# Register loads of one table entry per item, and TensorE's expert load between its two products, in a mixture-of-experts and attention kernel

## The reference

```python
x = x + 0.5 * ffn(layernorm(x))
x = x + attention(layernorm(x))          # 16 heads of 8, causal, rotary positions
x = x + 0.5 * ffn(layernorm(x))
```

```python
probs = softmax(xt @ Wr + br); gates = max(probs); idx = argmax(probs)      # per token
xn = layernorm(xt) * ln_g + ln_b
h = relu(xn @ W1[idx] + b1[idx])          # W1: 8 x 128 x 512
y = (h @ W2[idx] + b2[idx]) * gates       # W2: 8 x 512 x 128
```

## Time and profile before

| | us |
|---|---|
| runs of the kernel | 908.14, 914.18, 915.40 |
| median | 914.18 |
| span of the profiled execution | 855.6 |
| first item loop, in the profiled execution | about 44 to 132 |
| second item loop | about 759 to 846 |

### The profile page before, as it was taken

The page is one execution under the profiler, slowest core; times in us unless marked ns, Lnnn a source line. Parts: engine busy times, 40 slices in busy tenths (PEclk is TensorE's granted clock), DMA queues, the critical chain, the costliest instruction groups (busy, mean ns, idle before and its releaser), DMA issues. The chain is left out here.

```text
span 855.6 us, 17846 instructions
## 1 busy us (share of the span) xinstructions
PE 779.7 (91%) x5570; PEld 427.9 (50%) x5570; DVE 610.9 (71%) x1919; ACT 507.4 (59%) x1229; POOL 315.4 (37%) x603
## 2 busy tenths in 40 slices
PE   9889999887899999999999999999999997689995
PEld 8888896543233333333333333333333335579884
DVE  4657774698668777788878878788787722856663
ACT  2166651673247767667667766766777684146662
POOL 6177742475104223223322422331242231056753
PEclk8699999998569999999999999999999998789998
DMA  8721113065332033033113303312320001122110
GB/s 271 270 57 50 54 33 117 23 169 159 57 57 45 14 57 57 10 49 58 34 26 57 53 6 57 58 22 36 57 41 18 3 1 34 73 70 50 52 42 26
DMA packets 27989, 51.84 MB, mean 61 GB/s; under 512 B 7552, under 2 KB 19200, under 8 KB 26496
## 3 DMA queue, kind: packets, MB, share of 16 engines
q1 hardware_dynamic: 21296, 41.04, 20.7%
q0 software_dynamic: 4096, 8.69, 3.8%
q10 hardware_dynamic: 2512, 1.06, 0.5%
HBM read 35.40 MB, written 14.97 MB: 59 GB/s over the span
## 5 line engine op out<-in xcount | busy, mean ns | idle before, releaser
L1448 DVE CUSTOM_DVE_ANT_0 cst<-psS,mask_row 128x768 bf16<-128x768 f32 (+7 forms) x512 | 364.7, 756 | 100.2 <-PE psS L1308 97.6
L1412 ACT ACTIVATE prob<-psST 128x512 f32<-128x512 f32 (+3 forms) x750 | 317.3, 495 | 158.9 <-PE psST L1339 155.2
L1353 PE MATMUL a_psO<-prob,vs 128*32 128x512 f32 (+3 forms) x1536 | 166.7, 506 | 2.8 <-ACT prob L1412 1.7
L1532 POOL TENSOR_TENSOR a_gate<-a_zeros 1x1 f32<-1x1 f32 x128 | 23.7, 185 | 333.7 <-ACT prob L1412 333.7
L1339 PE MATMUL psST<-a_qs,ks 75*128 75x512 bf16 (+1 forms) x480 | 123.7, 327 | 5.9 <-ACT prob L1412 3.5
L1308 PE MATMUL psS<-ks,a_qs 72*128 72x512 bf16 (+2 forms) x480 | 119.0, 337 | 5.6 <-DVE a_rowmax L1448 5.5
L777 POOL DMA_INDIRECT tok<-rows,f_there_number x64 | 61.8, 966 | 86.0 <-DVE f_number L489 42.0
L1308 PEld LDWEIGHTS psS<-ks,a_qs 72*128 72x128 bf16 x480 | 35.6, 99 | 101.1 <-DVE a_rowmax L1448 33.0
L1308 PE MATMUL psS<-ks,qs 72*128 72x512 bf16 (+3 forms) x288 | 75.8, 354 | 6.7 <-DVE a_rowmax L1448 6.5
L1533 POOL TENSOR_SCALAR_AFFINE_SELECT prob<-prob 128x512 f32<-128x512 f32 x128 | 80.3, 627 | 0.0
L1339 PE MATMUL psST<-qs,ks 75*128 75x512 bf16 (+3 forms) x270 | 73.4, 346 | 2.7 <-ACT prob L1412 1.7
(11 more groups left out here) (183 smaller groups left out, 1066.1 us busy)
## 6 DMA issues: line engine op xcount, KB each, us to landing
a_qs<-q_split SPq DMA_DIRECT2D x60, 96.0 KB
rows<-tok SPq DMA_DIRECT2D x8, 536.0 KB, 4.9
ks<-k_split SPq DMA_DIRECT2D x32, 128.0 KB
qs<-q_split SPq DMA_DIRECT2D x36, 96.0 KB
q_split<-p_part SPq DMA_DIRECT2D x24, 128.0 KB, 2.4
k_split<-p_part SPq DMA_DIRECT2D x24, 128.0 KB, 2.4
ks<-k_split SPq DMA_DIRECT2D x16, 192.0 KB
tok<-x_after_first SPq DMA_DIRECT2D x4, 536.0 KB, 5.4
```

Source lines behind the costliest of these rows:

```text
L1353: last = nc.tensor.matmul(psO[32 * h:32 * h + 32, c0:c0 + w], vs[r][:, j, h, :], prob[:, u % RING, h, 0:w], start=(j == 0), stop=(u + 1 in ...
L1412: nc.scalar.activation(prob[:, u % RING, h, 0:w], score_buffer(s, u * QH + h)[:, 0:w], ACT.Exp, scale=SCALE).then_inc(exp_done, 1)
L1448: last = nc.vector.tensor_tensor_reduce(out=out[:, a * CH:a * CH + width], in0=ps[:, a * CH:a * CH + width], in1=mask_row[:, S - width:], ...
```

## The change

`VALUES` becomes 1: each load reads one entry, at each item, on all three engines. TensorE's load of the expert moves from the head of the step to between `turn_x(i + 1)` and `result(i - 1)`, and reads the entry of item i - 1, the one that `result` uses. The ring's entry is still read at the head of the step, ahead of `hidden(i)`. On DVE and ACT the places stay as they are. The number of load instructions of a table goes from 10 to 39 in each round. No arithmetic, wait or transfer is changed.

```diff
-LR, XR, VALUES = 12, 16, 4
+LR, XR, VALUES = 12, 16, 1
...
             def step(i):
                 if item(i):
                     values(mybir.EngineType.PE, item_ring, i, XR - 1, slot_of)
-                    values(mybir.EngineType.PE, item_expert, i, E - 1, expert)
                 hidden(i)
                 turn_x(i + 1)
+                if item(i - 1):
+                    values(mybir.EngineType.PE, item_expert, i - 1, E - 1, expert)
                 result(i - 1)
```

## The result

| | before | after |
|---|---|---|
| median of the runs, us | 911.16 (906.63 to 915.40, 4 runs) | 926.28 (922.40 to 927.47, 4 runs) |
| span of the profiled execution | 855.6 (a second one: 907.1) | 924.7 |

The changed kernel takes 1.0166 times as long, with a 95% interval of 1.0116 to 1.0216: +15.1 us, slower by over 1% as forecast, 7.7 us under the forecast time. The forecast took +19.9.

What follows compares the result with a forecast made beforehand. A per-item chain of latencies (turn, result, weigh, normalise; 2.11 us) was taken as the bound, nearly tied with TensorE's passes. 8.2 + 8.5 + 3.6 + 0.0 - 0.4 = +19.9 us on 914.2 gave 934, range 924 to 948.

Steps and rivals of the forecast that it cites:

- The circle: Latency chain of each item, turn, result, weigh, normalise, turn: TensorE's bare expert load lengthens it from 2.11 to 2.50 us.
- The length of a load: One value was put at 0.33 us, like four, plus 0.055 to the next instruction: 0.385 in all.
- An access 0.22 and the fixed part 0.11: Make-up of a TensorE load's time, taking four values as one access and three as three; one value then costs 0.33 us.
- The +1.2 us a round: `normalise` averages 0.384 us against 0.34 undisturbed; over 30 items all the excess was put on the chain of latencies.
- the forecast of 8.2 and 8.5: Growth in us from turn 1 to turn 31, first and second feed-forward round, to 75.6 us each.
- Items without a turn: Items 31 to 38, bounded by DVE's cycle, 2.4 us in the first round, 1.97 in the second: +3.6 and 0.0 us.
- The -0.4 at the head: Start of both rounds: the expert's first load no longer stands before the first `hidden`, about -0.2 us each.
- nothing outside the span changes: The 58.6 us between the profiled span and the runs' median stay, so a difference worked out on the span adds to the median.
- A: Rival: TensorE's expert load is covered, only 0.11 us of the ring's load shows, 2.2 us an item: 916 us; chance 0.08.
- B: Rival: a load of one value takes 0.03 us and fits under every cover: faster, 906 us; chance 0.02.
- C: Rival: one value costs what three do, 0.77 us: +41 and +28, 984 us; chance 0.07 including dearer loads in between.
- D: Rival: TensorE's granted clock falls as gaps grow to 0.26 us an item; +75 us or more at half clock; chance 0.02.

Runs made afterwards that it cites:

- plain transfers: Kernel before with POOL's indirect gathers and write-backs replaced by plain ones from SyncE, sorting left out: 849.99 us; with the changed loads 866.19 us.
- the order under the wait: Kernel before, four values a load, TensorE's two loads moved between `hidden` and `turn_x`: 911.33 us, 0.9996; without indirect transfers 845.37 us, 0.9250.

## Why the prediction was right, and where it was not

**The circle.** Right in mechanism, and nearly in size. TensorE's load stands bare between `normalise` and `result`, and each item of the loop grows by it. The slot was put at 0.385 and measures 0.36; the circle was put at 2.50 and measures 2.47. One sign came out otherwise: `result` was to start 0.59 after the turn's pass, and the rows have 0.41. The turn's recorded pass now starts 0.21 after `normalise` instead of 0.05. Counted from the end of `normalise` it is 0.62 against the predicted 0.05 + 0.21 + 0.385 = 0.645.

**The length of a load.** Mis-sized a little: 0.30 instead of 0.33. On 29 items that is 0.9 us a round. "An access 0.22 and the fixed part 0.11" gave a value near enough, but no run shows that this is how it is made up. The shortest load was taken for at least about 0.305; one value takes 0.28 on ACT.

The Trainium skill, "DMA: Bandwidth & Descriptors", section "Latency and other measured facts", has a floor of about 600 ns for a tensor_load. It doesn't hold here: the single-value loads above have medians of 278 to 310 ns on three engines, 78 in each row, and the estimate of 966 us by it was 40 us off. The Trainium skill, "Runtime: NRT & Kernel Launch", section "Instruction fetch mechanics", has some 200 ns a register, for loads from HBM. From SBUF, one register takes 0.30 us here and four take 0.33, so the cost doesn't go by the register, and that its estimate of 924 lies near the result is chance.

**`normalise`.** The +1.2 us a round didn't come: it averages 0.342 and 0.349 in the changed kernel. The prediction took the slowness of the earlier trace rows as given and put all of it on the circle. It goes away without a longer circle, too: with plain transfers and the loads of before it is gone, and with the write-backs alone indirect it is back (from 44 to 113 us in both):

```profile
L514 DVE TENSOR_SCALAR f_xn<-tok 128x128 f32<-128x128 f32 x30 | 10.2, 339 | 0.2 <-issue 0.2
```
```profile
L514 DVE TENSOR_SCALAR f_xn<-tok 128x128 f32<-128x128 f32 x30 | 11.4, 380 | 0.2 <-issue 0.2
```

In before all of the seven that take over 0.40 run while POOL issues an indirect transfer, and the 24 with none beside them average 0.339. So the slow ones go with POOL's indirect transfers; by what, no run shows. Without the 1.2, with loads 0.9 cheaper, and on the base of before with plain transfers (1.0 and 0.4 under the earlier trace rows), the forecast of 8.2 and 8.5 becomes 7.1 and 6.8, against the 6.8 and 7.2 measured there.

**Items without a turn.** DVE's cycle of 2.4 us in the first round is what the rows show. (The -0.4 at the head is too small to be read from single profiles.) The changed kernel's timeline of DVE:

```profile
156.98 0.28 DVE L529 TENSOR_TENSOR f_yb<-f_ps_number,w 128x128 f32<-128x128 f32 x1
...
158.84 0.61 DVE L522 TENSOR_SCALAR f_hidT<-f_ps_wide,f_w1s 128x128 f32<-128x128 f32 x2 [0.70 <-PE f_ps_rank L673]
159.36 0.28 DVE L529 TENSOR_TENSOR f_yb<-f_ps_rank,w 128x128 f32<-128x128 f32 x1
```

L529 to L529 is 2.38, and the stage takes 21.8 where 22.0 was forecast. In the second round 17.8 was forecast and 18.5 is measured (18.1 with plain transfers).

**The step that failed: "nothing outside the span changes".** The difference between median and profiled span, 58.6 us, was taken for time around the program. It was time of the program itself, most of it in the item loops, which the first profiled execution happened not to have. So the sum was made on a base without the long waits. By stages the turns cost +4.6 and +5.1 in the real kernels, against +6.8 and +7.2 without indirect transfers, some 2 us a round less. That loads go by unseen while an engine waits 7 us for a signal would explain it, but that is argued: each figure is a difference of two single profiles, and the medians, 15.1 and 16.2 us, can't be told apart within their intervals. So of the 19.9 forecast, 17.0 is there as cost by stages without indirect transfers, 13.7 by stages in the real kernels, and 15.1 in the medians. That the unforeseen waits left the forecast standing is in part luck; they could have hidden more of the cost.

**The rivals.** A (the load rides along, 916) fell with the turns at 2.47. B and C fell with 0.30 us a load. D: the clock did fall to 0.89, but in before just as much, and not through the loads: with plain transfers and the changed loads it is 1.00 from 46 to 114 us.

## What to carry to other kernels

A register load costs 0.3 us here whether it brings one value or four (three cost more), so what matters is how many there are and what they stand behind: straight behind a wait on which the circle of latencies turns, each is paid in full; ahead of such a wait it can be free, as in the turns that stay 2.11 apart. Before the sum is made, compare the span of the profiled execution with the runs: where they differ by 6%, profile once more, since the missing time may be a wait inside the loop that hides or changes what is being priced. And try a small gain also with the larger noise taken away, as here the order under the wait showed 5 us without the indirect transfers, with intervals that overlap, and nothing with them.

## What the runs showed that was not expected

**Signals of TensorE that arrive late beside indirect transfers.** The changed kernel's timeline from 51.9 us, with POOL, TensorE, ACT and DVE:

```profile
51.92 0.95 POOL L778 DMA_INDIRECT tok<-rows,f_there_number  x1 [0.30 <-issue]
...
52.19 0.42 PE L654 MATMUL f_ps_half<-cst,f_xn 128*128 128x128 f32 x1
...
53.17 0.95 POOL L778 DMA_INDIRECT tok<-rows,f_there_number  x1 [0.31 <-issue]
...
58.17 0.94 POOL L778 DMA_INDIRECT tok<-rows,f_there_number  x1 [0.30 <-issue]
...
60.28 0.61 DVE L522 TENSOR_SCALAR f_hidT<-f_ps_wide,f_w1s 128x128 f32<-128x128 f32 x2 [10.31 <-remote]
60.32 0.46 ACT L727 ACTIVATE f_xnT<-f_ps_half,gb 128x128 f32<-128x128 f32 x1 [9.10 <-remote]
```

The turn's pass ends at 52.61 by the records. The copy on ACT that waits for it starts at 60.32, 7.7 us later, 1.2 us after POOL's row of gathers, one each 1.25 us, has ended at 59.11. DVE starts in the same moment. "remote" means that the profile finds no instruction of this core that released them. The waits of before, first loop, show the same three (total, times, longest):

```profile
ACT f_xnT L726 <- remote: 19.9, 3, 11.2
...
DVE f_hidT L522 <- remote: 13.4, 4, 7.5
...
DVE f_yb L529 <- remote: 7.7, 4, 3.9
```

The long intervals stand in items 1 to 4, where twelve gathers are issued in a row, and in items 12 to 22, where most items have a gather and a write-back. In items 5 to 11 (one gather an item) and from 23 on (write-backs alone) there are none. That the indirect transfers are needed for them is shown: without them before runs in 850 us instead of 913 (49 of the 60 us between the two profiles are in the turns), and no wait of its first loop is "remote"; with the write-backs alone indirect it is 856. How they hold a signal up isn't shown, and neither is why the first profiled execution of before, with the same transfers, had none of it. Those kernels also leave POOL's issuing of descriptors and the order of the rows away, so a shared path of POOL and the semaphores, and the load on the DMA engines, can't be told apart.

The record of the landings goes with the waits as well. Every transfer raises its semaphore by 16 steps, 2048 for the 128 gathers and write-backs. With plain transfers the trace has all 2048 and in the first profile of before 2009, but in the second only 975, and in the changed kernel 1138; the other transfers have 3632 each time. The view of DMA issues shows it, as it gives a time to landing (2.6 us) only where the steps are complete; the first profile of before, then the second:

```profile
tok<-rows,f_there_number POOLq DMA_INDIRECT x64, 2.6
```
```profile
tok<-rows,f_there_number POOLq DMA_INDIRECT x64
```

With only the write-backs indirect 1591 are there and no wait is "remote", so missing records alone don't make a wait. Whether they have the same cause as the late signals isn't shown.

**A load of three is dearer than one of four.** Three values take 0.77 to 0.86 us on TensorE, four 0.33 and one 0.30. The three are the last entries of a table, but that is not it: read one by one in the changed kernel, they take 0.30 each on TensorE. No run varied the count further.
